# Values of a window-attention block made channel-major, turned in 32x32 blocks and passed through DRAM

## Chip, cores and metric

One Trainium2 chip, one of its cores. The metric is the device time of one execution in microseconds; the median of three runs of the kernel before is 2936.64 us.

## Reference, cut to what matters

A Swin block on x of shape (16, 192, 56, 56) in float32: layer norm over the 192 channels, cyclic shift by 3, windows of 7x7 = 49 tokens, attention with 6 heads of 32 channels, projection, second layer norm, an MLP with a hidden width of 768, and the input added at the end.

```python
qkv = jnp.einsum('bnc,oc->bno', xw, qkv_w) + qkv_b
qkv = qkv.reshape(Bw, N, 3, HEADS, dh)
q, k, v = (qkv[:, :, 0], qkv[:, :, 1], qkv[:, :, 2])
attn = jnp.einsum('bnhd,bmhd->bhnm', q, k) * scale
attn = jax.nn.softmax(attn, axis=-1)
out = jnp.einsum('bhnm,bmhd->bnhd', attn, v).reshape(Bw, N, C)
out = jnp.einsum('bnc,oc->bno', out, proj_w) + proj_b
```

## The kernel before

The work is cut into 128 units, each one row of eight windows: 8 x 49 = 392 tokens (T), four pairs of windows with 98 tokens (TP) each. Every engine runs a written-out loop over steps `t`; in each step it works on several units at once, `u[lag]` being unit `t - lag`. The order inside a step is fixed by hand in the `step` function of each engine, and semaphores tie the engines together. TensorE starts a unit (lag 0) with the products of queries, keys and values. The labels of the steps differ by engine: VectorE takes the values of a unit out of PSUM at its lag 3, while SyncE moves them at its lag 4 and GpSimd's lags are one lower than VectorE's.

To keep float32 precision, each operand is a high part in fp32r and a low part that is the rest. A product of 192 input channels is then five products: `x_h` with high and low weights, `x_l` with high weights, and the tile `x_r` (the last 64 channels' high part on partitions 0 to 63, their low part on 64 to 127) with `w_rh` and `w_rl`. `five` (lines 325 to 329) has the channels of the output on partitions and 392 columns; `five_tokens` (lines 335 to 339) has the 98 tokens of a pair on partitions and 192 columns. The values use `five_tokens`, four times a unit, 20 products in all, in the PSUM banks `vt` 0 and 1.

VectorE copies the values from PSUM to the tile `vs` in two instructions (`v_out`, line 1071): [98 tokens, pair, 192 channels]. SyncE's `spread` (line 453) moves them from `vs` to `vbd` in four transfers, for each window of a pair and each head of a pair of heads. Each has 49 partitions and runs of 32 floats, so 49 x 12 = 588 runs of 128 bytes. `vbd` holds blocks with the tokens of one head on partitions 0 to 48 and those of the next on 64 to 112, each beside zeros. `weighted` (line 607), the last work of TensorE's step, reads it one step later.

All transfers of the steady state are issued by SyncE, in this order in its step t:

```python
load_groups(t)      # xg, line 395
stats_in(t - 2)     # bc from DRAM, line 412
spread(t - 4)       # vbd, line 453
stats_out(t - 1)    # mean_rstd to DRAM, lines 404, 405; waits for GpSimd
store(t - 7)        # out, lines 419, 420; waits for GpSimd's residual
load(...)           # xt, lines 386, 387
```

GpSimd's step, in order: `scaled_probs(3)`, `hidden_lo_last`, `scaled_probs(0)`, `rstd(0)`, `less_mean_rest` (line 1233), `times_rstd_rest` (line 1237), `rstd(1)` (lines 1222 and 1226), `scaled_probs(1)`, `residual` (line 1254), `scaled_probs(2)`. `rstd(1)` feeds VectorE's `normalise` (line 993), and `residual` releases SyncE's `store`.

Of the kernel before, what the change touches and what calls it, by code (L numbers as in the profile page):

```python
# [101 lines left out]
def swin_block_program(nc, x, n1w, n1b, qkv_wt, qkv_b, proj_wt, proj_b, n2w, n2b,  # L102
                       fc1_wt, fc1_b, fc2_wt, fc2_b, out):
    ctx = ExitStack()
    with ctx:
# [28 lines left out]
        wq = [sb(f"wq_{p}", [128, NQ], F32R) for p in ("mh", "ml", "rh", "rl")]  # L134
        wp = [sb(f"wp_{p}", [128, CR + C], F32R) for p in ("mh", "ml", "rh", "rl")]
        w1 = [sb(f"w1_{p}", [128, NF], F32R) for p in ("mh", "ml", "rh", "rl")]
        w2h = sb("w2h", [128, MT, C], F32R)
        w2l = sb("w2l", [128, MT, CM], F32R)
        w2r = sb("w2r", [128, MT, 128], F32R)
# [40 lines left out]
        half_k = sb("half_k", [128, 2])  # L180
        bk = sb("bk", [128, 2])

        vbd = sb("vbd", [128, 2, 2, PAIRS, 3, WP])
        vs = sb("vs", [TP, 2, PAIRS, C])
# [52 lines left out]
        s_vs = sem("values_in_sbuf")  # L237
# [58 lines left out]
        def last_read(name, i, v):  # L296

            if name in ("x2", "o"):
                return s_lo[name], v, 3, 2 * i
            if name == "ln2":  # L300
                return s_norm, v, PAIRS, 2 * i + 1
            if name == "vt":
                return s_vs, v, 2, i
# [76 lines left out]
        def _(sp):  # L380
# [59 lines left out]
            sp.dma_start(b2[:, 0:1], fc2_b[0:CM].rearrange("(p a) -> p a", a=1)).then_inc(s_rest, 16)  # L440
            sp.dma_start(b2[0:CR, 1:2], fc2_b[CM:C].rearrange("(p a) -> p a", a=1)).then_inc(s_rest, 16)

            def spread(u):

                sp.wait_ge(s_vs, nth(u, 2, 1))
                if u > 1:

                    sp.wait_ge(s_pe["o"], nth(u - 2, 1, 0))
                src = vs[:, u % 2].rearrange("p j (a e d) -> p (j a) e d", a=3, e=2)
                dst = vbd[:, u % 2].rearrange("p i j a d -> p i (j a) d")  # L450
                for wi in range(2):
                    for e in range(2):
                        sp.dma_start(dst[WP * e:WP * e + N, wi, :, DH * e:DH * e + DH],
                                     src[N * wi:N * wi + N, :, e, :]).then_inc(s_vbd[u % 2], 16)

            for t in range(UNITS + 7):
                if t < UNITS:
                    if t > 2:
                        load_groups(t)
                    if 1 < t < AHEAD:  # L460
                        load(0, t)
                if 0 <= t - 2 < UNITS:
                    if t - 2 > 0:
# [24 lines left out]
        def _(pe):  # L488
# [102 lines left out]
            def weighted(u, j):  # L591
                if j == 0:
                    pe.wait_ge(s_vbd[u % 2], nth(u // 2, VMOVES, VMOVES - 1))
                    claim(u, [("o", 0), ("o", 1)], (s_ptc, PAIRS, 0))
                else:
                    claim(u, [], (s_ptc, PAIRS, j))


                for wi, p in ((0, 0), (0, 1), (1, 0), (1, 1), (0, 2), (1, 2)):
                    if p < 2:  # L600
                        w = 2 * j + wi
                        ps = bank("o", 0)[WP * p:WP * p + WP, N * w:N * w + N]
# [4 lines left out]
                    last = nc.tensor.matmul(ps, vbd[0:KP, u % 2, wi, j, p, :], pt[:, j, block, N * side:N * side + N],  # L607
                                            start=True, stop=True)
                if j == PAIRS - 1:
                    last.then_inc(s_pe["o"], 1)  # L610
# [5 lines left out]
                if u == 0 and tile == 4:  # L616
                    hidden_bias_products()

            def values(u, j):
                c, cc = j // 2, j % 2  # L620
                if cc == 0:
                    claim(u, [("vt", c)], (s_lo["x1"], 2, 1))
                pairs = [p[:, TP * j:TP * j + TP] for p in x1]
                last = five_tokens(bank("vt", c)[0:TP, cc * C:(cc + 1) * C], wq, pairs)
                if cc == 1:
                    last.then_inc(s_pe["vt"], 1)

            def step(t, k, it):
                u = units(t)
                if u[0] is not None:  # L630
                    values(u[0], 0)
                if u[4] is not None:
                    fc2_lo(u[4], 3)
                if u[0] is not None:
# [2 lines left out]
                    fc2_lo(u[4], 4)  # L637
                    fc2_lo(u[4], 5)
                if u[0] is not None:
                    values(u[0], 1)  # L640
                    values(u[0], 2)
                if u[3] is not None:
                    fc1(u[3], 0)
                if u[0] is not None:
                    values(u[0], 3)
                if u[3] is not None:
                    fc1(u[3], 1)
                if u[0] is not None:
# [237 lines left out]
        def _(dve):  # L886
# [9 lines left out]
            def split(n, w, raw, cols, nw, scaled):  # L896
# [14 lines left out]
                dve.wait_ge(s_scaled, scaled)  # L911
                nc.vector.tensor_tensor(w[1][:, :], sm_[:, 0:cols], w[0][:, :].bitcast(F32), ALU.subtract)

                low = CR if n == 1 else 128
                nc.vector.tensor_tensor(w[3][0:low, :], sr_[0:low, 0:cols], w[2][0:low, :].bitcast(F32), ALU.subtract).then_inc(s_split, 1)
                return scaled
# [149 lines left out]
            def v_out(u, c):  # L1066
                if u > 1:

                    dve.wait_ge(s_vbd[u % 2], nth(u // 2 - 1, VMOVES, VMOVES - 1))
                dve.wait_ge(s_pe["vt"], nth(u, 2, c))  # L1070
                nc.vector.tensor_copy(vs[:, u % 2, 2 * c:2 * c + 2, :], bank("vt", c)[0:TP, 0:2 * C].rearrange("p (j n) -> p j n", j=2)).then_inc(s_vs, 1)

            def step(t, k, it):
                u = units(t)
# [95 lines left out]
                if u[3] is not None:  # L1170
                    less_max(u[3], 0)
                    row_max(u[3], 1)
                if u[5] is not None:
# [5 lines left out]
                if u[2] is not None:  # L1179
                    if u[2] > 0:  # L1180
                        lo_part("x1", u[2], 1)
                if u[3] is not None:
                    row_max(u[3], 2)
                if u[0] is not None:
# [23 lines left out]
        def _(pool):  # L1208
# [30 lines left out]
            def hidden_lo_last(u):  # L1239
# [16 lines left out]
            def step(t, k, it):  # L1256
# [10 lines left out]
                if u[1] is not None:  # L1267
                    if u[1] > 0:
                        less_mean_rest(u[1], (k - 1) % SLOTS)
                    if u[1] > 0:  # L1270
                        times_rstd_rest(u[1])
                if u[4] is not None:
                    rstd(1, u[4])
                if u[3] is not None:
# [35 lines left out]
```

## Time and profile before

| | |
|---|---|
| median of three runs | 2936.64 us (2935.59 to 3475.99) |
| profiled execution | 2936.91 us |
| its span in the trace | 2935.1 us |
| TensorE busy | 2889.1 us (98%) |
| VectorE busy | 2629.3 us (90%) |
| ScalarE busy | 2690.1 us (92%) |
| GpSimd busy | 1363.0 us (46%) |

The profiled execution is 0.3 us from the median. Its span is the time between the first and the last record of the trace; 1.8 us of the execution lie around it. A busy share is the share of the span in which an engine had an instruction under way; the chain of work that ended last says which engine's work set the end. The DMA share is the mean busy share of the core's 16 DMA engines.

### The profile page before, as it was taken

Reading aid. Unit: us, or ns where it says so; the run is one execution under the profiler, and the core shown is the slowest. Engines: PE = TensorE matmul, PEld = TensorE weight load, DVE = VectorE, ACT = ScalarE, POOL = GpSimd, SP = SyncE. Lnnn points to the kernel's source line nnn. Section 1 sums busy time; section 2 is a strip of 40 time slices with the busy share of each in tenths; the row PEclk is TensorE's granted clock in tenths of the full one; section 3 lists DMA queues with packets and bytes.
Section 4 is the critical chain, followed back from the end, with each engine's and each line's share of the span. In section 5 each row is a group of like instructions: output and inputs, shape, how many; then the busy total and the mean of one; then the engine's idle time right before and its main releaser. Section 6 shows DMA issues by size and latency. Waiting matters only on the chain.

```text
span 2935.1 us, 74792 instructions
## 1 busy us (share of the span) xinstructions
PE 2889.1 (98%) x26284; PEld 2820.0 (96%) x26284; DVE 2629.3 (90%) x7211; ACT 2690.1 (92%) x5500; POOL 1363.0 (46%) x1549
## 2 busy tenths in 40 slices
PE   5999999999999999999999999999999999999998
PEld 5999999999999999999999999999999999999998
DVE  7899999999999999999999999999999999999985
ACT  2899999999999999999999999999999999999996
POOL 3444444444445444444444444444445444444442
PEclk9999999999999999999999999999999999999999
DMA  5333333333333333333333333333333333333321
GB/s 110 56 78 76 71 71 76 77 68 76 79 70 71 74 79 68 74 78 72 68 76 80 68 72 78 74 68 76 80 69 72 76 77 67 76 73 75 69 62 26
DMA packets 645586, 213.10 MB, mean 73 GB/s; under 512 B 500835, under 2 KB 628580, under 8 KB 645220
## 3 DMA queue, kind: packets, MB, share of 16 engines
q1 hardware_dynamic: 641284, 206.65, 32.2%
q8 instruction: 217, 3.56, 0.6%
q10 hardware_dynamic: 3936, 1.68, 0.3%
q14 instruction: 149, 1.22, 0.2%
HBM read 130.69 MB, written 38.94 MB: 58 GB/s over the span
## 4 chain that ended last, share of the span: by engine, by line
PE 97%; SPq 1%; DVE 1%; DMA 0%; POOL 0%; ACT 0%; issue 0%; POOLq 0%; DVEq 0%; ACTq 0%
PE psum L325 7%; PE psum L329 7%; PE psum L327 7%; PE psum L328 7%; PE psum L326 7%; PE psum L607 7%; PE psum L581 6%; PE psum L561 5%; PE psum L572 5%; PE psum L562 5%; PE psum L563 5%; PE psum L573 5%; PE psum L587 4%; PE psum L335 4%; PE psum L337 3%; PE psum L339 3%
## 5 line engine op out<-in xcount | busy, mean ns | idle before, releaser
L1249 POOL TENSOR_TENSOR pr<-pr,rc 98x294 f32<-98x294 f32 x512 | 386.4, 764 | 378.3 <-DVE rc L1064 378.3
L763 ACT ACTIVATE hh<-psum,b 128x392 fp32r<-128x392 f32 x768 | 451.5, 588 | 43.3 <-PE psum L573 34.7
L766 ACT ACTIVATE hf<-psum,b 128x392 f32<-128x392 f32 x768 | 451.4, 588 | 6.3
L1222 POOL TENSOR_TENSOR ve<-mv,eps 104x4 f32<-104x4 f32 (+1 forms) x256 | 80.9, 316 | 759.8 <-DVE mv L988 759.8
L1243 POOL TENSOR_TENSOR hl<-hf,hh 128x392 fp32r<-128x392 f32 x128 | 224.0, 1750 | 370.5 <-ACT hf L766 370.5
L1028 DVE TENSOR_TENSOR hl<-hf,hh 128x392 fp32r<-128x392 f32 x640 | 347.9, 559 | 4.0 <-ACT hf L766 4.0
L1051 DVE TENSOR_REDUCE mx<-psum 98x6 f32<-98x294 f32 x512 | 232.2, 454 | 128.4 <-PE psum L582 124.5
L561 PE MATMUL psum<-hh,w2h 128*128 128x392 f32 x768 | 272.1, 354 | 0.0
L325 PE MATMUL psum<-x_h,w_mh 128*128 128x392 f32 x768 | 270.2, 352 | 0.7 <-DVE pr L1056 0.7
L581 PE MATMUL psum<-km,qm 128*98 128x98 f32 x2048 | 262.5, 251 | 7.7 <-DVE xn L993 3.4
L720 ACT ACTIVATE pt<-psum 113x294 f32<-113x294 f32 x512 | 206.3, 403 | 69.2 <-PE psum L587 69.0
L572 PE MATMUL psum<-hl,w2h 128*128 128x392 f32 x768 | 264.4, 344 | 0.3 <-POOL hl L1243 0.3
L329 PE MATMUL psum<-x_r,w_rl 128*128 128x392 f32 x768 | 262.7, 342 | 0.0
L327 PE MATMUL psum<-x_l,w_mh 128*128 128x392 f32 x768 | 262.0, 341 | 0.0
L562 PE MATMUL psum<-hh,w2l 128*128 128x392 f32 x768 | 262.0, 341 | 0.0
L328 PE MATMUL psum<-x_r,w_rh 128*128 128x392 f32 x768 | 260.9, 340 | 0.0
L326 PE MATMUL psum<-x_h,w_ml 128*128 128x392 f32 x768 | 260.8, 340 | 0.0
L573 PE MATMUL psum<-hl,w2h 128*64 128x392 f32 x768 | 259.8, 338 | 0.0
L563 PE MATMUL psum<-hh,w2r 128*128 128x392 f32 x768 | 259.2, 338 | 0.0
L980 DVE BATCH_NORM_STATS2 st<-psum 98x6 f32<-98x192 f32 x512 | 184.0, 359 | 74.8 <-PE psum L339 70.7
L581 PEld LDWEIGHTS psum<-km,qm 128*98 128x98 f32 x2048 | 238.5, 167 | 12.4 <-issue 6.3
L1056 DVE TENSOR_TENSOR pr<-psum,mx 98x294 f32<-98x294 f32 x512 | 234.1, 457 | 4.2
(144 smaller groups left out, 10394.9 us busy)
## 6 DMA issues: line engine op xcount, KB each, us to landing
bc<-mean_rstd SPq DMA_DIRECT2D x128, 392.0 KB, 3.7
vbd<-vs SPq DMA_DIRECT2D x512, 73.5 KB
xg<-in_x SPq DMA_DIRECT2D x368, 96.0 KB, 2.5
xt<-in_x SPq DMA_DIRECT2D x112, 194.5 KB, 2.7
out<-xt SPq DMA_DIRECT2D x112, 194.5 KB, 1.9
xt<-in_x SPq DMA_DIRECT2D x112, 97.2 KB, 2.5
out<-xt SPq DMA_DIRECT2D x112, 97.2 KB, 2.1
mean_rstd<-mv SPq DMA_DIRECT2D x384, 1.0 KB
```

Of the source, the lines that this page charges most:

```text
L325: nc.tensor.matmul(ps, wmh[:, c0:c0 + m], xh, start=True, stop=False)
L326: nc.tensor.matmul(ps, wml[:, c0:c0 + m], xh, start=False, stop=False)
L327: nc.tensor.matmul(ps, wmh[:, c0:c0 + m], xl, start=False, stop=False)
L328: nc.tensor.matmul(ps, wrh[:, c0:c0 + m], xrr, start=False, stop=False)
L329: return nc.tensor.matmul(ps, wrl[:, c0:c0 + m], xrr, start=False, stop=True)
L561: nc.tensor.matmul(ym, w2h[:, m, 0:CM], hh[:, b, :], start=a, stop=False)
L562: nc.tensor.matmul(ym, w2l[:, m, :], hh[:, b, :], start=False, stop=False)
L572: nc.tensor.matmul(ym, w2h[:, m, 0:CM], hl[:, b, :], start=False, stop=z)
L573: nc.tensor.matmul(yx[0:CR], w2h[:, m, CM:C], hl[:, b, :], start=False, stop=z, skip_group_check=True).then_inc(s_pe["fc2"], 1)
L581: nc.tensor.matmul(ps[:, TP * wi:TP * wi + TP], qm[:, w, :], km[:, w, :], start=True, stop=True)
L763: nc.scalar.activation(hh[:, m % HB, :], bank("fc1", m)[:, 0:T], ACT.Gelu, bias=b1[:, m:m + 1]).then_inc(s_hh, 1)
L766: nc.scalar.activation(hf[:, m % HB, :], bank("fc1", m)[:, 0:T], ACT.Gelu, bias=b1[:, m:m + 1]).then_inc(s_gelu, 1)
```

## The change

The values are computed with channels on partitions. `values_rest` makes the last 64 channels in three products: a weight tile `wv_m` holds the high weights in its columns 0 to 63 and the low ones in 64 to 127, `wv_r` likewise, so that the partitions 0 to 63 of the result have one part of the sum and 64 to 127 the other. `values_main` makes the first 128 channels with `five`. That is eight products of 392 columns.

VectorE no longer copies: `v_out` turns 32x32 blocks from PSUM to SBUF (`vt_r`, then `vt_m`), [128 channels, 8 windows, 2 blocks of 32 tokens]. A window has 49 tokens, so its second block begins at token 17 and repeats 15 of them. After it the partition within a block is the token and the last dimension the channel of a head.

SyncE's `low_part` moves the lower half of `vt_r` to `vt_l` on partitions 0 to 63. GpSimd's `last_values` adds it. `values_to_dram` writes both tiles to a DRAM tensor `by_token`, and `spread` reads `vbd` from it one step later, in four transfers: for each head of a pair, 32 tokens and then the 17 that are left. Each moves runs of 128 bytes, as before: 32 x 24 = 768 runs and 17 x 24 = 408.

In VectorE's step, `lo_part("x1", 1)` (line 1022, `x_r`) moves ahead of `lo_part("x2", 0)`, `less_max(1)` and `hidden_lo(4)`. In SyncE's step `low_part(t - 3)` follows `spread(t - 4)`, and `values_to_dram(t - 3)` follows `stats_out(t - 1)`.

```diff
             def spread(u):
-                sp.wait_ge(s_vs, nth(u, 2, 1))
+                sp.wait_ge(s_vd, 16 * 2 * (u + 1))
                 if u > 1:
                     sp.wait_ge(s_pe["o"], nth(u - 2, 1, 0))
-                src = vs[:, u % 2].rearrange("p j (a e d) -> p (j a) e d", a=3, e=2)
-                dst = vbd[:, u % 2].rearrange("p i j a d -> p i (j a) d")
-                for wi in range(2):
-                    for e in range(2):
-                        sp.dma_start(dst[WP * e:WP * e + N, wi, :, DH * e:DH * e + DH],
-                                     src[N * wi:N * wi + N, :, e, :]).then_inc(s_vbd[u % 2], 16)
+                of_pair = by_token[u % 2].rearrange("(p e t) w b d -> e b t w p d", p=3, e=2)
+                for e in range(2):
+                    dst = vbd[:, u % 2, :, :, DH * e:DH * e + DH]
+                    sp.dma_start(dst[WP * e:WP * e + DH], of_pair[e, 0]).then_inc(s_vbd[u % 2], 16)
+                    sp.dma_start(dst[WP * e + DH:WP * e + N], of_pair[e, 1, 2 * DH - N:DH]).then_inc(s_vbd[u % 2], 16)
...
+            def low_part(u):
+                sp.wait_ge(s_vt, nth(u, 2, 0))
+                if u > 0:
+                    sp.wait_ge(s_vsum, nth(u - 1, 1, 0))
+                sp.dma_start(vt_l[:, :, :, :], vt_r[CR:128, u % 2]).then_inc(s_vlow, 16)
+            def values_to_dram(u):
+                sp.wait_ge(s_vt, nth(u, 2, 1))
+                if u > 1:
+                    sp.wait_ge(s_vbd[u % 2], 16 * 4 * (u // 2))
+                sp.dma_start(by_token[u % 2, 0:CM], vt_m[:, u % 2]).then_inc(s_vd, 16)
+                sp.wait_ge(s_vsum, nth(u, 1, 0))
+                sp.dma_start(by_token[u % 2, CM:C], vt_r[0:CR, u % 2]).then_inc(s_vd, 16)
...
                 if 0 <= t - 4 < UNITS:
                     spread(t - 4)
+                if 0 <= t - 3 < UNITS:
+                    low_part(t - 3)
...
                         stats_out(t - 1)
+                if 0 <= t - 3 < UNITS:
+                    values_to_dram(t - 3)
...
+            def values_main(u):
+                claim(u, [("vt", 1)])
+                five(bank("vt", 1)[:, 0:T], wq, 0, CM, [p[:, :] for p in x1]).then_inc(s_pe["vt"], 1)
+            def values_rest(u):
+                claim(u, [("vt", 0)], (s_lo["x1"], 2, 0))
+                ps = bank("vt", 0)[:, 0:T]
+                nc.tensor.matmul(ps, wv_m[:, :], x1[0][:, :], start=True, stop=False)
+                nc.tensor.matmul(ps, wv_m[:, :], x1[1][:, :], start=False, stop=False)
+                pe.wait_ge(s_lo["x1"], nth(u, 2, 1))
+                nc.tensor.matmul(ps, wv_r[:, :], x1[2][:, :], start=False, stop=True).then_inc(s_pe["vt"], 1)
...
                 dve.wait_ge(s_pe["vt"], nth(u, 2, c))
-                nc.vector.tensor_copy(vs[:, u % 2, 2 * c:2 * c + 2, :], bank("vt", c)[0:TP, 0:2 * C].rearrange("p (j n) -> p j n", j=2)).then_inc(s_vs, 1)
+                blocks = bass.AP(psum, BANK_OF["vt", c] * 512, [[8 * 512, 128], [N, NW], [N - DH, 2], [1, DH]])
+                nc.vector.transpose((vt_r, vt_m)[c][:, u % 2], blocks).then_inc(s_vt, 1)
...
+            def last_values(u):
+                pool.wait_ge(s_vlow, 16 * (u + 1))
+                nc.gpsimd.tensor_tensor(vt_r[0:CR, u % 2], vt_r[0:CR, u % 2], vt_l[:, :, :, :], ALU.add).then_inc(s_vsum, 1)
...
                     if u[1] > 0:
                         times_rstd_rest(u[1])
+                if u[2] is not None:
+                    last_values(u[2])
                 if u[4] is not None:
                     rstd(1, u[4])
```

In TensorE's step, `values_rest` stands where the first pair of the values stood, `values_main` where the second and third stood, and the fourth is gone. VectorE makes `wv_m` and `wv_r` once, in the prologue, with four small instructions. `weighted` reads `vbd` by window instead of by pair and window.

## Rows read from the trace of the kernel before

**Rows 1.** The page: busy time of each engine, and the last chain by engine.

```profile
PE 2889.1 (98%) x26284; PEld 2820.0 (96%) x26284; DVE 2629.3 (90%) x7211; ACT 2690.1 (92%) x5500; POOL 1363.0 (46%) x1549
...
PE 97%; SPq 1%; DVE 1%; DMA 0%; POOL 0%; ACT 0%; issue 0%; POOLq 0%; DVEq 0%; ACTq 0%
```

**Rows 2.** The last chain in order of time: start, length, what; one unit apart.

```profile
1741.03 1.54 PE psum L607 x48
1763.41 1.54 PE psum L607 x48
```

**Rows 3.** Waits: engine and line, releaser: us in total, times, longest.

```profile
POOL ve L1222 <- DVE mv L988: 759.8, 255, 12.1
...
DVE mx L1051 <- PE psum L582: 124.5, 125, 2.2
DVE st L980 <- PE psum L339: 70.7, 134, 1.9
```

**Rows 4.** Waits of the SyncE queue, same columns.

```profile
SPq L417 <- POOL xt L1254: 948.4, 128, 16.1
```

**Rows 5.** Timeline of TensorE, 1500 to 1524: start us, length us, operation.

```profile
1500.64 0.25 PE L335 MATMUL psum<-wq_mh,x_h 128*98 128x192 f32 x1
...
1501.09 0.36 PE L325 MATMUL psum<-x_h,w_mh 128*128 128x392 f32 x1
...
1502.00 0.34 PE L325 MATMUL psum<-x_h,wq_mh 128*128 128x392 f32 x1
...
1502.89 0.25 PE L335 MATMUL psum<-wp_mh,o_h 128*98 128x192 f32 x1
```

**Rows 6.** Timeline of VectorE, 1500 to 1530; idle time before in brackets.

```profile
1500.59 0.53 DVE L1071 COPY vs<-psum 98x384 f32<-98x384 f32 x1
...
1502.53 0.97 DVE L959 STREAM_TRANSPOSE xtok<-xg 128x768 f32<-128x768 f32 x1
1503.98 0.37 DVE L980 BATCH_NORM_STATS2 st<-psum 98x6 f32<-98x192 f32 x1 [0.49 <-PE psum L339]
...
1513.35 0.47 DVE L1051 TENSOR_REDUCE mx<-psum 98x6 f32<-98x294 f32 x1 [1.00 <-PE psum L582]
...
1515.25 0.57 DVE L1022 TENSOR_TENSOR x_l<-psum,x_h 128x392 fp32r<-128x392 f32 x1 [0.21 <-ACT x_h L720]
...
1516.69 1.26 DVE L1022 TENSOR_TENSOR x_r<-yr,x_r 64x392 fp32r<-64x392 f32 x1
...
1520.43 0.75 DVE L999 TENSOR_TENSOR x_r<-psum,x_r 64x196 fp32r<-64x196 f32 x2
```

**Rows 7.** Timeline of VectorE in the prologue.

```profile
53.55 0.56 DVE L1022 TENSOR_TENSOR x_r<-yr,x_r 64x392 fp32r<-64x392 f32 x1
```

**Rows 8.** Timeline of GpSimd, 1500 to 1530.

```profile
1503.14 1.04 POOL L1237 TENSOR_TENSOR yr<-yr,bc 64x392 f32<-64x392 f32 x1
1507.93 0.43 POOL L1222 TENSOR_TENSOR ve<-mv,eps 98x4 f32<-98x4 f32 x1 [3.76 <-DVE mv L988]
...
1510.27 1.02 POOL L1254 TENSOR_TENSOR xt<-yr,xt 64x392 f32<-64x392 f32 x1
```

**Rows 9.** Windows of 0.5 us: length, GpSimd busy, PEclk, DMA share, GB/s.

```profile
1519.00:1519.50 0.50, 0.00 (x0) 1.00 0.80 196
...
1521.00:1521.50 0.50, 0.11 (x1) 1.00 0.66 270
...
1523.50:1524.00 0.50, 0.50 (x1) 1.00 0.55 85
...
1528.00:1528.50 0.50, 0.00 (x0) 1.00 0.00 0
```

**Rows 10.** DMA issues: count, KB each, median us to landing.

```profile
bc<-mean_rstd SPq DMA_DIRECT2D x128, 392.0 KB, 3.7
vbd<-vs SPq DMA_DIRECT2D x512, 73.5 KB
xg<-in_x SPq DMA_DIRECT2D x368, 96.0 KB, 2.5
```

**Rows 11.** Timeline of the SyncE queue, 1480 to 1530: start, issue time, transfer.

```profile
1488.98 0.36 SPq L419 DMA_DIRECT2D out<-xt  x1
...
1496.65 4.85 SPq L453 DMA_DIRECT2D vbd<-vs  x4
...
1511.36 0.36 SPq L419 DMA_DIRECT2D out<-xt  x1
...
1520.31 3.77 SPq L453 DMA_DIRECT2D vbd<-vs  x4
```

More of the change, by code:

```diff
@@ L136, in swin_block_program @@
         w1 = [sb(f"w1_{p}", [128, NF], F32R) for p in ("mh", "ml", "rh", "rl")]
+        wv_m = sb("wv_m", [128, 128], F32R)
+        wv_r = sb("wv_r", [128, 128], F32R)
         w2h = sb("w2h", [128, MT, C], F32R)
@@ L181, in swin_block_program @@
         bk = sb("bk", [128, 2])
-        vbd = sb("vbd", [128, 2, 2, PAIRS, 3, WP])
-        vs = sb("vs", [TP, 2, PAIRS, C])
+        vbd = sb("vbd", [128, 2, NW, 3, WP])
+        vt_m = sb("vt_m", [128, 2, NW, 2, DH])
+        vt_r = sb("vt_r", [128, 2, NW, 2, DH])
+        vt_l = sb("vt_l", [CR, NW, 2, DH])
+        by_token = nc.dram_tensor("values_by_token", [2, C, NW, 2, DH], F32)
         pr = sb("pr", [TP, PAIRS, HEADS * WP])
@@ L236, in swin_block_program @@
         s_qkv = sem("qkv_in_sbuf")
-        s_vs = sem("values_in_sbuf")
+        s_vt = sem("values_by_token")
+        s_vlow = sem("low_part_of_last_values_moved")
+        s_vsum = sem("last_values_summed")
+        s_vd = sem("values_in_dram")
         s_vbd = [sem(f"vbd_ready_{i}") for i in range(2)]
@@ L302, in last_read @@
             if name == "vt":
-                return s_vs, v, 2, i
+                return s_vt, v, 2, i
             if name == "qkv":
@@ L606, in weighted @@
                     block, side = (wi, p) if p < 2 else (2, wi)
-                    last = nc.tensor.matmul(ps, vbd[0:KP, u % 2, wi, j, p, :], pt[:, j, block, N * side:N * side + N],
+                    last = nc.tensor.matmul(ps, vbd[0:KP, u % 2, 2 * j + wi, p, :], pt[:, j, block, N * side:N * side + N],
                                             start=True, stop=True)
@@ L617, in qkv @@
                     hidden_bias_products()
[L619 to L626, printed above, removed]
+            def values_main(u):
[8 more added lines that the diff above has]
+                nc.tensor.matmul(ps, wv_r[:, :], x1[2][:, :], start=False, stop=True).then_inc(s_pe["vt"], 1)
             def step(t, k, it):
@@ L630, in step @@
                 if u[0] is not None:
-                    values(u[0], 0)
+                    values_rest(u[0])
                 if u[4] is not None:
@@ L639, in step @@
                 if u[0] is not None:
-                    values(u[0], 1)
-                    values(u[0], 2)
+                    values_main(u[0])
                 if u[3] is not None:
                     fc1(u[3], 0)
-                if u[0] is not None:
-                    values(u[0], 3)
                 if u[3] is not None:
@@ L912, in split @@
                 nc.vector.tensor_tensor(w[1][:, :], sm_[:, 0:cols], w[0][:, :].bitcast(F32), ALU.subtract)
+                if n == 0:
+                    for pair, raw_, of in ((wv_m, sm_, w[0]), (wv_r, sr_, w[2])):
+                        nc.vector.tensor_copy(pair[:, 0:CR], of[:, CM:C].bitcast(F32))
+                        nc.vector.tensor_tensor(pair[:, CR:128], raw_[:, CM:C], of[:, CM:C].bitcast(F32), ALU.subtract)
                 low = CR if n == 1 else 128
@@ L1067, in v_out @@
                 if u > 1:
-                    dve.wait_ge(s_vbd[u % 2], nth(u // 2 - 1, VMOVES, VMOVES - 1))
+                    dve.wait_ge(s_vd, 16 * 2 * (u - 1))
                 dve.wait_ge(s_pe["vt"], nth(u, 2, c))
-                nc.vector.tensor_copy(vs[:, u % 2, 2 * c:2 * c + 2, :], bank("vt", c)[0:TP, 0:2 * C].rearrange("p (j n) -> p j n", j=2)).then_inc(s_vs, 1)
+                blocks = bass.AP(psum, BANK_OF["vt", c] * 512, [[8 * 512, 128], [N, NW], [N - DH, 2], [1, DH]])
+                nc.vector.transpose((vt_r, vt_m)[c][:, u % 2], blocks).then_inc(s_vt, 1)
             def step(t, k, it):
@@ L1172, in step @@
                     row_max(u[3], 1)
+                if u[2] is not None:
+                    if u[2] > 0:
+                        lo_part("x1", u[2], 1)
                 if u[5] is not None:
@@ L1178, in step @@
                     hidden_lo(u[6], 4)
-                if u[2] is not None:
-                    if u[2] > 0:
-                        lo_part("x1", u[2], 1)
                 if u[3] is not None:
@@ L1271, in step @@
                         times_rstd_rest(u[1])
+                if u[2] is not None:
+                    last_values(u[2])
                 if u[4] is not None:
```

## The prediction

> **What bounds the kernel now.** I read the page first: TensorE is busy for 98% of the span, and 97% of the chain that ended last is its work [rows 1]. Then the chain in time: `weighted` comes back after exactly 22.38 us (1763.41 - 1741.03) [rows 2], so 128 units make 2865 us, and some 70 us are prologue and drain. TensorE hardly waits for anybody. The waits tell who has room: VectorE waits 124.5 us for scores and 70.7 us for the projection, some 1.5 us a unit; GpSimd waits 759.8 us for VectorE's means [rows 3]; SyncE's queue waits 948.4 us, 7.4 us a unit, for GpSimd's `residual` [rows 4]. The first question is what TensorE saves, the second whether anything that the change puts behind SyncE, GpSimd or a DMA engine makes a loop longer than 22.38 us.
>
> **What TensorE saves.** In the steady pitch five products of 192 columns take 0.45 us (1501.09 - 1500.64) and five of 392 columns 0.89 us (1502.89 - 1502.00) [rows 5]: 0.090 and 0.178 us each. 20 x 0.090 = 1.80 us of values become 8 x 0.178 = 1.42. That is 0.38 us a unit, 48 us in all; a little of the changeover between narrow and wide products goes too (0.91 instead of 0.89 us for the wide group behind a narrow one [rows 5]), so up to 56 us. If nothing else bound, the period would be 22.0 us.
>
> **VectorE.** Two copies of 384 elements (0.53 us [rows 6]) become two block turns of 512. The nearest row is the turn of 768 elements from SBUF, 0.97 us [rows 6]; in proportion 0.65, and at most 0.97 if PSUM is slower. So +0.1 to +0.45 each; I take +0.15, and 0.3 a unit. VectorE's idle time in one step is 0.49 + 1.00 + 0.21 = 1.70 us [rows 6]; 0.4 of it goes with TensorE's shorter period, 0.3 (at most 0.9) with the turns. 0.4 us or more are left: it doesn't become the bound. Moving `x_r` forward costs nothing and may give 0.7 us back: the same instruction takes 1.26 us in the steady state, behind GpSimd's work on `hl`, but 0.56 us in the prologue [rows 6, 7], and in its new place it would start before that work. It delays three instructions by 0.6 to 1.3 us; `x_r` on line 999, which follows all three, keeps its time at 1521.2 [rows 6]. `values_main` takes over its PSUM bank at just about that time; a stall of 0 to 0.2 us a unit there is possible, and I take 0. The four instructions in the prologue are 1 us.
>
> **GpSimd.** `last_values` adds 64x512 elements; line 1237 adds 64x392 in 1.04 us [rows 8], so 1.04 x 512/392 = 1.36 us. It stands in a gap of 3.76 us between 1504.2 and 1507.9 [rows 8] and is free if its data are there by about 1506.5. If they aren't, `rstd(1)`, the probabilities and `residual` are queued behind it on GpSimd; `normalise` on VectorE waits for the first, SyncE's `store` for the last.
>
> **The read-back, the term that decides.** Before, each of the four transfers has 49 partitions. A stretch in which hardly anything else moves shows them at 85 GB/s and a DMA share of 0.55, where the `xg` transfers (32 partitions) reach 196 GB/s and 0.80 [rows 9]. So 49 partitions don't use all 16 DMA engines. If a transfer is cut into equal groups of partitions over at most 16 engines, 49 = 7 x 7 goes to seven. Then the pace is 85 GB/s / 128 bytes / 7 = 95 runs a microsecond on an engine, 10.5 ns a run, while the record of a run lasts 0.55 x 16 x 500 ns / 332 runs = 13.3 ns: neighbours overlap, which is how seven engines show a share over 7/16. Cut by the same arithmetic, 32 partitions go to 16 engines, 48 runs each; but 17 is a prime and over 16, so all its 408 runs go to one engine. Per unit that engine gets 48 + 408 + 48 + 408 = 912 runs in a row, where the busiest had 336 before. The number of runs and of bytes stays as it was; only their spread over engines changes.
>
> The Trainium skill, "DMA: Bandwidth & Descriptors", section "Why a DMA increments its semaphore by 16 and not by 1", has this as a rule: the number of engines is the largest one up to 16 that divides the slowest dimension of both sides, and they are the lowest-numbered. The measured share and rate of 49 partitions agree with its seven; that 17 gives one, no run here shows yet. By the rule the sum is the one below; with an even spread it would be the first rival's.
>
> The price of a run read from DRAM by one engine isn't in the trace. From below it is the 10.5 ns of SBUF. From above: `xg` with runs of 512 bytes (196 GB/s, share 0.80) has 33 ns a run and `bc` with 3136 bytes (270 GB/s, 0.66) 123 ns [rows 9, 10]; a line through both gives 20.3 ns at 128 bytes, with 16 engines sharing the DRAM. I take 13.3 ns, the length of a record of the same size. 912 runs last 9.6, 12.1 or 18.5 us.
>
> **Why that isn't hidden.** `vbd` itself has time: `weighted` stands at the end of the step. But `low_part` is issued behind `spread` on the same queue, and a share of it goes over the crowded engine, behind the 912 runs. So there is a loop of SyncE, that engine and GpSimd:
>
> - from `store`'s first issue to `spread`'s first: 20.31 - 11.36 = 8.95 us in one step, 96.65 - 88.98 = 7.67 in the one before [rows 11]; 8.3.
> - from the issue to the first runs, with the `bc` transfer in front: the pure stretch at 1523.50 is already under way at 1523.0 or before, issue at 1520.31 [rows 9, 11]; 2.5.
> - the 912 runs: 12.1 (9.6 to 18.5).
> - `low_part`'s own rows and its landing: an estimate of 0.8 from transfers that land 2.5 us after their issue [rows 10], most of which is gone by then.
> - `last_values`: 1.36.
> - GpSimd from `rstd(1)` to the end of `residual`, and `store`'s issue: 11.36 - 7.93 = 3.43 [rows 8, 11].
>
> Sum: 8.3 + 2.5 + 12.1 + 0.8 + 1.36 + 3.43 = 28.5 us (26.0 to 34.9), over 22.38 and over 22.0. The wait for `residual`, 7.4 us a unit [rows 4], is the slack that it eats, and the saving of TensorE doesn't show. If SyncE can't hand over 408 runs to one engine at once, `low_part` is issued up to 2 us later, within the range. The other three additions (the writes to DRAM in rows of 2048 bytes, their waits) stand behind `low_part`; `values_to_dram` waits for the sum, which comes 3.4 us ahead of the release of `store`, and has landed long before the next `spread`.
>
> Against the profiled execution (span 2935.1, 2936.9 in all, the median's 2936.6): 127 x (28.5 - 22.38) = 777, so 3714; I say 3710. With 26.0 it is 3400, with the shorter SyncE stretch and landing 3250; with 34.9 4530.
>
> **Rivals.**
> - *The 17 partitions are spread.* If they go over several engines as evenly as 49 do, the read-back takes 2352 runs at 85 GB/s, 3.5 us, `low_part` lands by 1505 in the frame of the rows, and all is hidden: TensorE's saving alone counts, 2937 - 52 = 2885. For it: nothing in the rows shows how 17 are cut. Against: the low share of 49. This is the case on the other side; it decides if the runs on the busiest engine last under about 5 us (22.0 - 16.4 = 5.6 us for the whole stretch).
> - *The added step isn't hidden even so.* With spread transfers, but `low_part` landing after 1506.5, `last_values` pushes `rstd(1)` back by up to its 1.36 us; VectorE's remaining 1.0 us takes most of it. 128 x 0.4 on top of 2885 is 2936.
> - *DRAM is dearer than the line.* At 25 ns a run 22.8 us, period 39.2 us, 2937 + 127 x 16.8 = 5070. For it: all these reads hit DRAM in pieces of 128 bytes. Against: the line through two rows stays under it although 16 engines shared the DRAM there.
>
> **Chances.** Forecast (one engine, 10 to 21 ns) 0.74; spread and hidden 0.11; spread and late 0.05; dearer DRAM 0.10. The range 3250 to 4700 takes the forecast with its bounds and the near edge of the last case, and leaves the two spread cases and the far edge out. A measurement of this kernel can tell 2% from no change: faster by more than 2% would be under 2878, which only the spread case could reach with a changeover gain: 0.04. Within 2%: 0.12. Slower: 0.84.
>
> **What would show it.** Right: TensorE with an idle stretch in each step and a period of 26 to 35 us; GpSimd waiting at `last_values` for a DMA; a stretch of some 10 us in each unit with a DMA share near 1/16 (0.06 to 0.1) and about 10 GB/s; VectorE waiting for GpSimd's `rs`. The number of products of 392 columns up by 1024, those of 192 down by 2560, at the same pitch. Turns of about 0.65 us. Wrong: if the share stays near 0.55 during `spread`, the step about one engine fails; if the share is low but GpSimd doesn't wait, the step about the order on the queue does. The prediction would also be off if TensorE's clock fell in its idle stretches, which the rows, with a granted clock of 1.00 throughout [rows 9], don't show.

## The result, and the profile after

| | before | after |
|---|---|---|
| median | 2936.11 us | 3278.9 us |
| ratio | | 1.117, 95% interval 1.116 to 1.118 |
| span of the profiled execution | 2935.1 us | 3280.7 us |
| period of a unit | 22.38 us | 25.1 us (mean) |

One of the four runs of the kernel before took 3475.99 us and is left out of the ratio; the others lie between 2934 and 2937. The change makes the kernel 343 us slower. The forecast was 3710 us (774 more), with a range of 3250 to 4700. The whole difference is in the period: 127 x (25.12 - 22.38) = 348 us.

The page of the kernel after, the busy times and the chain that ended last by engine; they answer to [rows 1].

```profile
PE 2961.8 (90%) x24748; PEld 2824.3 (86%) x24748; DVE 2740.6 (84%) x7215; ACT 2693.7 (82%) x5500; POOL 1344.3 (41%) x1677
...
SPq 53%; DMA 21%; POOL 16%; PE 5%; issue 5%; ACT 0%; DVE 0%; POOLq 0%; DVEq 0%; ACTq 0%
```

TensorE's work of the last chain has gone from 97% to 5%. The set of things that now follow on one another is SyncE's queue, a DMA and GpSimd. The waits of the engines and then of SyncE's queue say the same; they answer to [rows 3, 4].

```profile
POOL vt_r L1292 <- DMA vt_l<-vt_r: 774.8, 126, 8.1
...
DVE xn L1033 <- POOL rs L1270: 339.7, 123, 5.4
```

```profile
SPq L428 <- POOL xt L1303: 326.9, 127, 13.0
SPq L470 <- POOL vt_r L1292: 109.1, 121, 2.4
```

GpSimd waits 774.8 us, 6.1 us a unit, for the low part to land, and behind it VectorE waits 340 us for `rs`. SyncE's wait for `residual` has shrunk from 948.4 us to 326.9. So the loop that the prediction names is there. One turn of it in SyncE's timeline (start, issue time, transfer), which answers to [rows 11]:

```profile
1504.22 0.64 SPq L481 DMA_DIRECT2D vbd<-values_by_token  x1
1504.91 0.68 SPq L482 DMA_DIRECT2D vbd<-values_by_token  x1
1505.64 4.31 SPq L481 DMA_DIRECT2D vbd<-values_by_token  x1
1509.99 0.64 SPq L482 DMA_DIRECT2D vbd<-values_by_token  x1
1510.73 3.58 SPq L460 DMA_DIRECT2D vt_l<-vt_r  x1
...
1520.41 0.35 SPq L430 DMA_DIRECT2D out<-xt  x1
...
1530.43 0.63 SPq L481 DMA_DIRECT2D vbd<-values_by_token  x1
```

The lines 481 are the transfers of 32 partitions, 482 those of 17, 460 is the low part. The transfer behind each one of 17 partitions takes 4.31 and 3.58 us to issue, where its like takes 0.64 and some 0.5; I call the extra time a hold. GpSimd in the same stretch, to be held against [rows 8]:

```profile
1516.19 1.28 POOL L1292 TENSOR_TENSOR vt_r<-vt_r,vt_l 64x512 f32<-64x512 f32 x1 [5.63 <-DMA vt_l<-vt_r]
1517.43 0.19 POOL L1266 TENSOR_TENSOR ve<-mv,eps 98x4 f32<-98x4 f32 x1
...
1519.33 1.00 POOL L1303 TENSOR_TENSOR xt<-yr,xt 64x392 f32<-64x392 f32 x1
```

The sum starts at 1516.19, 1.9 us after the low part's issue has ended, and `rstd(1)` (line 1266), the probabilities and `residual` (line 1303) follow without a gap; `store` is issued at 1520.41. Taken over some 100 turns between 200 and 2750 us, the three stretches are, from `store` to the first read-back 8.80 us, from there to the sum 12.05, from the sum to `store` 4.27: together 25.12, the period.

The windows of 1 us (length, TensorE busy, PEclk, DMA share, GB/s), which answer to [rows 9]:

```profile
1508.00:1509.00 1.00, 1.00 (x8) 1.00 0.09 14
1509.00:1510.00 1.00, 1.00 (x10) 1.00 0.09 14
1510.00:1511.00 1.00, 1.00 (x13) 1.00 0.20 33
1511.00:1512.00 1.00, 1.00 (x9) 1.00 0.55 86
1512.00:1513.00 1.00, 1.00 (x11) 1.00 0.09 14
...
1515.00:1516.00 1.00, 1.00 (x8) 1.00 0.68 129
...
1543.00:1544.00 1.00, 0.73 (x5) 1.00 0.64 246
1544.00:1545.00 1.00, 0.00 (x0) 1.00 0.00 0
1545.00:1546.00 1.00, 0.25 (x2) 0.91 0.21 55
1546.00:1547.00 1.00, 1.00 (x8) 0.50 0.42 92
...
1549.00:1550.00 1.00, 1.00 (x8) 0.89 0.28 45
```

Between two transfers of 32 partitions (the 0.55 at 1511) the share is 0.09 and the rate 14 GB/s. I read that as the crowded engine alone: 128 bytes / 14 GB/s = 9.1 ns a run. The profile doesn't name the DMA engines; the experiments below vary how many runs one of them would get. In windows of 0.25 us the 14 GB/s last until 1510.5, and until 1514.75 behind the second transfer of 17 partitions, so each held issue (to 1509.95 and to 1514.31) ends about 0.5 us or more before the last of the runs.

### The profile page after: what moved, and what is told of

Same layout as the page of the kernel before. It is cut to its first block, busy times and chain, and to the rows that moved or that the text cites. A ratio compares the mean times of both kernels' runs of the same rounds, so it can differ in the third digit from the quotient of the medians.

```text
span 3280.7 us, 72362 instructions
## 1 busy us (share of the span) xinstructions
PE 2961.8 (90%) x24748; PEld 2824.3 (86%) x24748; DVE 2740.6 (84%) x7215; ACT 2693.7 (82%) x5500; POOL 1344.3 (41%) x1677
## 3 DMA queue, kind: packets, MB, share of 16 engines
q14 instruction: 155, 1.27, 0.2%
## 4 chain that ended last, share of the span: by engine, by line
SPq 53%; DMA 21%; POOL 16%; PE 5%; issue 5%; ACT 0%; DVE 0%; POOLq 0%; DVEq 0%; ACTq 0%
DMA vt_l<-vt_r 21%; SPq L481 18%; SPq L406 10%; SPq L397 5%; SPq L482 5%; POOL vt_r L1292 5%; SPq L431 4%; SPq L398 4%; SPq L430 4%; POOL rs L1270 4%; POOL xt L1303 4%; POOL pr L1298 2%; SPq L423 2%; POOL ve L1266 1%; PE psum L639 0%
## 5 line engine op out<-in xcount | busy, mean ns | idle before, releaser
L1298 POOL TENSOR_TENSOR pr<-pr,rc 98x294 f32<-98x294 f32 x512 | 344.0, 681 | 490.3 <-DVE rc L1104 490.3
L1033 DVE TENSOR_SCALAR xn<-psum,mv,rs 98x192 f32<-98x192 f32 x512 | 218.5, 469 | 339.8 <-POOL rs L1270 339.7
L1292 POOL TENSOR_TENSOR vt_r<-vt_r,vt_l 64x512 f32<-64x512 f32 x128 | 168.0, 1312 | 774.8 <-DMA vt_l<-vt_r 774.8
L613 PE MATMUL psum<-km,qm 128*98 128x98 f32 x2048 | 284.0, 264 | 146.2 <-DVE xn L1033 137.3
L1068 DVE TENSOR_TENSOR hl<-hf,hh 128x392 fp32r<-128x392 f32 x640 | 369.1, 577 | 24.0 <-ACT hf L801 13.3
L639 PE MATMUL psum<-pt,vbd 113*64 113x49 f32 x6144 | 206.1, 223 | 95.7 <-DVE pr L1096 95.7
L639 PEld LDWEIGHTS psum<-pt,vbd 113*64 113x64 f32 x6144 | 192.6, 138 | 111.6 <-issue 107.9
L593 PE MATMUL psum<-hh,w2h 128*128 128x392 f32 x768 | 281.7, 367 | 0.0
L619 PE MATMUL psum<-ident,pr 98*128 98x98 f32 x1536 | 232.0, 264 | 40.5 <-POOL pr L1298 39.7
```

Of the source, the lines that this page charges most:

```text
L593: nc.tensor.matmul(ym, w2h[:, m, 0:CM], hh[:, b, :], start=a, stop=False)
L613: nc.tensor.matmul(ps[:, TP * wi:TP * wi + TP], qm[:, w, :], km[:, w, :], start=True, stop=True)
L639: last = nc.tensor.matmul(ps, vbd[0:KP, u % 2, 2 * j + wi, p, :], pt[:, j, block, N * side:N * side + N], start=True, stop=True)
L1068: nc.vector.tensor_tensor(hl[:, b, :], hf[:, b, :], hh[:, b, :].bitcast(F32), ALU.subtract).then_inc(s_hl, 1)
L1292: nc.gpsimd.tensor_tensor(vt_r[0:CR, u % 2], vt_r[0:CR, u % 2], vt_l[:, :, :, :], ALU.add).then_inc(s_vsum, 1)
L1298: nc.gpsimd.tensor_tensor(probs(j), probs(j), each, ALU.mult).then_inc(s_prob, 1)
```

## Experiments

In the table, "middle" is the mean time from the first read-back issue to the sum on GpSimd, and "SyncE's work" the period less its waits for semaphores, so its issues and whatever holds them. Both are worked out from the timelines and waits of each profile; "busiest" counts the 128-byte runs of a unit on the busiest engine, by equal groups of partitions; it is worked out and not read from a profile. A single partition is counted by its next dimension, the 8 windows, which no run measures by itself (with all of it on one engine the 150 would be 192, the 531 552). Where the low part goes ahead of the read-back, the middle no longer holds all of the read-back. The diffs leave out the semaphore increments and counts and the conditions around calls.

| kernel | busiest | period | middle | SyncE's work | time | ratio to before |
|---|---|---|---|---|---|---|
| before | 336 | 22.38 | | 14.2 | 2936 | 1 |
| after | 912 | 25.12 | 12.05 | 21.6 | 3279 | 1.117 |
| 32, 16 and 1 | 150 | 22.12 | 6.95 | 16.2 | 2910 | 0.991 (0.9895 to 0.9925) |
| low part first | 912 | 22.68 | 4.81 | 21.7 | 2982 | 1.017 (1.015 to 1.018) |
| 31 and 18 | 1584 | 31.4 | 18.43 | | 4069, one run | |
| before, cut at 32 | 912 | 22.38 | | 20.2 | 2943, one run | |
| no low part | 912 | 22.22 | | 21.5 | 2913 | 0.992 (0.990 to 0.994) |
| both cures | 150 | 22.14 | 2.53 | | 2909 | 0.991 (0.989 to 0.992) |
| old place of x_r | 150 | 22.63 | 7.04 | | 2973 | 1.013 (1.011 to 1.014) |
| one seventeen | 531 | 23.23 | 9.79 | 19.4 | 3052 | 1.040 (1.038 to 1.042) |
| behind the means | 912 | 23.64 | 3.30 | 22.9 | 3093 | 1.053 (1.052 to 1.055) |
| before, x_r early | 336 | | | | 2937 | 1.0006 (0.9996 to 1.0015) |
| seventeens apart | 912 | 23.64 | 6.16 | 22.9 | 3095 | 1.054 (1.052 to 1.056) |

**Is it the 17 partitions?** The read-back in 32, 16 and 1 partitions:

```diff
-    sp.dma_start(dst[WP * e + DH:WP * e + N], of_pair[e, 1, 2 * DH - N:DH])
+    sp.dma_start(dst[WP * e + DH + 1:WP * e + N], of_pair[e, 1, 2 * DH - N + 1:DH])
+    sp.dma_start(dst[WP * e + DH:WP * e + DH + 1], of_pair[e, 1, 2 * DH - N:2 * DH - N + 1])
```

> The changed kernel with the read-back cut into 32, 16 and 1 partitions per head instead of 32 and 17: the same runs of 128 bytes, two more transfers a unit. Theory (the 816 runs of the two 17-partition transfers go over one DMA engine, and the low part waits behind them): no engine has more than some 150 runs in a row, the 12.05 us between the first read-back issue and the sum on GpSimd fall to 5 or 6, the loop of 8.8 + 6 + 4.3 = 19 us is shorter than TensorE's step, period 22.0 to 22.4, time 2885 to 2930. Rival (short reads from DRAM are dear on whatever engines): the stretch stays near 12 us and the time at 3279. Rival (the added round trip and sum are dear by themselves): 3150 or more.

2909.56 us: 369 us less than the changed kernel, with the same runs and two more transfers, and 0.9% faster than before. SyncE's timeline of this kernel:

```profile
1507.84 0.63 SPq L481 DMA_DIRECT2D vbd<-values_by_token  x1
1508.52 0.66 SPq L482 DMA_DIRECT2D vbd<-values_by_token  x1
1509.22 0.71 SPq L483 DMA_DIRECT2D vbd<-values_by_token  x1
...
1512.13 0.53 SPq L460 DMA_DIRECT2D vt_l<-vt_r  x1
...
1521.04 0.36 SPq L430 DMA_DIRECT2D out<-xt  x1
```

No issue is held: 0.63, 0.66, 0.71, and 0.53 for the low part, which the sum follows at 1514.51, 1.85 us after the issue has ended, as in the changed kernel. So neither short reads from DRAM nor the added round trip is dear by itself.

**The slope.** 31 and 18 partitions instead of 32 and 17:

```diff
-    sp.dma_start(dst[WP * e:WP * e + DH], of_pair[e, 0])
-    sp.dma_start(dst[WP * e + DH:WP * e + N], of_pair[e, 1, 2 * DH - N:DH])
+    sp.dma_start(dst[WP * e:WP * e + DH - 1], of_pair[e, 0, 0:DH - 1])
+    sp.dma_start(dst[WP * e + DH - 1:WP * e + N], of_pair[e, 1, 2 * DH - N - 1:DH])
```

> The changed kernel with the read-back cut into 31 and 18 partitions per head. 31 is a prime too, so 744 runs each would go over one engine, and 18 over nine: 1584 runs in a row on the busiest engine instead of 912, with as many runs in all. Theory, at the 9.1 ns a run that the profile of the change shows: 672 x 9.1 ns = 6.1 us more a unit, period 31.2 us, time near 4055. Rival (the number of runs in all counts, or their size): 3279.

4069 us against 4055 expected; the middle is 6.4 us longer, 672 runs x 9.5 ns. SyncE's timeline (481: 31 partitions, 482: 18):

```profile
1520.35 0.73 SPq L481 DMA_DIRECT2D vbd<-values_by_token  x1
1521.13 7.40 SPq L482 DMA_DIRECT2D vbd<-values_by_token  x1
1528.59 0.66 SPq L481 DMA_DIRECT2D vbd<-values_by_token  x1
1529.29 6.96 SPq L482 DMA_DIRECT2D vbd<-values_by_token  x1
```

744 runs x 9.1 ns are 6.8 us. Here a transfer of 18 partitions carries the hold of the one before it, 7.40 and 6.96 us, for an issue of 0.7. The same count of runs and bytes gives 2910, 3279 or 4069 us, by the number of partitions of a transfer (the first has two transfers more). That the groups are equal and 31 and 17 go to one engine explains all three. (The kernel with 31 and 18 ran once.)

**SBUF or DRAM?** The kernel before, with its moves cut the same way:

```diff
-    sp.dma_start(dst[WP * e:WP * e + N, wi, :, DH * e:DH * e + DH],
-                 src[N * wi:N * wi + N, :, e, :]).then_inc(s_vbd[u % 2], 16)
+    for a, z in ((0, DH), (DH, N)):
+        sp.dma_start(dst[WP * e + a:WP * e + z, wi, :, DH * e:DH * e + DH],
+                     src[N * wi + a:N * wi + z, :, e, :]).then_inc(s_vbd[u % 2], 16)
```

> The kernel before with its moves from SBUF cut into 32 and 17 partitions: eight transfers instead of four, 912 runs in a row on one engine, and no GpSimd step behind them. Theory: hidden, 2936 within 1%; the windows show a DMA share of 0.09. Their rate is the price of a run from SBUF: 14 GB/s (9.1 ns) if DRAM is no dearer than SBUF, over it if DRAM is dearer. Rival (one crowded engine delays the whole queue): 3000 or more.

2943 us in one run, with the period at 22.38 us as before. Windows of 0.5 us (length, PEclk, DMA share, GB/s):

```profile
1507.50:1508.00 0.50, 1.00 0.09 14
1508.00:1508.50 0.50, 1.00 0.09 14
```

14 GB/s from SBUF too: a run from DRAM takes no longer. And the kernel before has room for all of it, though SyncE's work rises from 14.2 to 20.2 us a unit.

**Who waits: the place in the queue.** The low part ahead of the read-back:

```diff
+                if 0 <= t - 3 < UNITS:
+                    low_part(t - 3)
                 if 0 <= t - 4 < UNITS:
                     spread(t - 4)
-                if 0 <= t - 3 < UNITS:
-                    low_part(t - 3)
```

> The changed kernel with the low part issued ahead of the read-back on SyncE's queue; the 17-partition transfers stay. Theory: the crowded engine still works 8.3 us a unit (DMA share 0.09 at 14 GB/s), but nothing that GpSimd needs stands behind it, so the loop is open: period 22.0 to 22.4, time 2885 to 2940. Rival (the read-back is itself late for the weighted sums, or delays the next unit's loads and means): 3000 or more.

2982 us, a miss: most of the loss is gone, but 72 us stay over 2910. GpSimd now waits 349 us for the broadcast means instead of the 46 of the changed kernel. I took it for their place behind the runs and put the read-back behind the means' writes as well:

```diff
-                spread(t - 4)
                 low_part(t - 3)
                 stats_out(t - 1)
+                spread(t - 4)
```

> The changed kernel with the read-back (17-partition transfers kept) issued behind the low part and behind the means' way to DRAM. With the low part alone in front the time was 2982, and GpSimd waited 349 us for the broadcast means, whose writes stood behind the runs. Theory (the crowded engine costs only what stands behind it): with the means in front too, that wait falls under 80 us and the time to 2905 to 2935. Rival (SyncE's queue itself is full, since it is held 4 us by one such transfer): 2960 or more, with SyncE no longer waiting for GpSimd's residual.

3093 us: worse, the rival. The wait for the means grew to 488 us. SyncE's timeline, the second 17 and what follows it:

```profile
1524.80 0.63 SPq L482 DMA_DIRECT2D vbd<-values_by_token  x1
1525.54 3.62 SPq L468 DMA_DIRECT2D values_by_token<-vt_m  x1
```

and SyncE's waits of the same run:

```profile
SPq L428 <- POOL xt L1303: 38.8, 4, 13.5
```

SyncE hardly waits for `residual` any longer (38.8 us in all): its queue is the bound. The values' write to DRAM, 0.34 us of issue otherwise, takes 3.62. So the hold isn't on the low part; it falls on whatever SyncE issues next. The 72 us of the reordering before this one aren't isolated by any run: SyncE's work is 21.7 us of 22.68 there, and the first write of the means is the issue that is held, up to 3.9 us.

**Half of the cure.** Only the second head's 17 partitions become 16 and 1:

```diff
-    sp.dma_start(dst[WP * e + DH:WP * e + N], of_pair[e, 1, 2 * DH - N:DH])
+    if e == 0:
+        sp.dma_start(dst[WP * e + DH:WP * e + N], of_pair[e, 1, 2 * DH - N:DH])
+    else:
+        sp.dma_start(dst[WP * e + DH + 1:WP * e + N], of_pair[e, 1, 2 * DH - N + 1:DH])
+        sp.dma_start(dst[WP * e + DH:WP * e + DH + 1], of_pair[e, 1, 2 * DH - N:2 * DH - N + 1])
```

> Only the second head of a pair read back in 32, 16 and 1 partitions; the first keeps 32 and 17. The busiest engine has 531 runs instead of 912, 3.5 us less at 9.1 ns. By the sum of the loop: 8.8 + (12.05 - 3.5) + 4.3 = 21.7 us, just under TensorE's 22.1, so 2910 to 2935: half of the cure gives nearly all of the gain. If each 17-partition transfer costs its share whatever the bound: near 3095, half of the way from 3279 to 2910.

3052 us, a miss: the sum of the loop had the wrong middle, 8.6 instead of 9.79, and 4.3 instead of 4.7 behind it. I had taken off 381 runs x 9.1 ns = 3.5 us. The held issue of one turn:

```profile
1514.13 3.82 SPq L485 DMA_DIRECT2D vbd<-values_by_token  x1
```

Its median over the run is 4.05 us, 3.4 more than the 0.62 of its like. By holds the table nearly adds up: 6.95 with none, + 3.4 for one held issue - 0.7 for one issue less is 9.65 (9.79 measured). In the changed kernel the two held issues take 4.07 and 3.69 us on average, 3.4 and 3.2 over their own, so 6.95 + 6.6 - 1.4 is 12.15 (12.05 measured).

**Cutting the loop elsewhere.** Without `low_part` and `last_values`; the values of the last 64 channels lack their low part:

```diff
-                if 0 <= t - 3 < UNITS:
-                    low_part(t - 3)
...
-                sp.wait_ge(s_vsum, nth(u, 1, 0))
...
-                if u[2] is not None:
-                    last_values(u[2])
```

> The changed kernel, 17-partition transfers kept, without the low part's move and without its sum on GpSimd, so the values of the last 64 channels lack their low part. Theory (the crowded engine costs time only through what GpSimd waits for behind it): 912 runs still take 8.3 us on one engine, but the loop is cut; TensorE bounds, period 22.1 us as with 32, 16 and 1 partitions, 2900 to 2920. Rival (the crowded queue delays loads, means or the values themselves, as it did to the means when the low part went first): 2960 or more.

2913 us with all 912 runs on one engine. So with the loop over GpSimd cut in this way the time is 4 us over that of 32, 16 and 1 partitions, not 369. (That kernel still has the low part and its sum; a kernel without either and with 32, 16 and 1 wasn't run.) But SyncE's work is 21.5 us of 22.2: it is nearly full.

**Both cures, and the holds apart.** The read-back in 32, 16 and 1 (the first diff) with the low part ahead of it (the diff of the low part first):

> Read-back in 32, 16 and 1 partitions, and the low part ahead of it. Theory (TensorE bounds already with the first edit): 2900 to 2915, no gain over 2910. Rival (what is left of GpSimd's wait for the low part, 124 us, costs time): 2885 to 2895.

2909 us: nothing more to gain there. Then the same four transfers as in the changed kernel, the two of 17 partitions issued apart:

```diff
                 for e in range(2):
-                    dst = vbd[:, u % 2, :, :, DH * e:DH * e + DH]
-                    sp.dma_start(dst[WP * e:WP * e + DH], of_pair[e, 0])
-                    sp.dma_start(dst[WP * e + DH:WP * e + N], of_pair[e, 1, 2 * DH - N:DH])
+                    sp.dma_start(vbd[WP * e:WP * e + DH, u % 2, :, :, DH * e:DH * e + DH], of_pair(u)[e, 0])
...
+            def seventeen(u, e):
+                sp.dma_start(vbd[WP * e + DH:WP * e + N, u % 2, :, :, DH * e:DH * e + DH],
+                             of_pair(u)[e, 1, 2 * DH - N:DH])
...
+                if 0 <= t - 4 < UNITS:
+                    seventeen(t - 4, 0)
                 if 0 <= t - 3 < UNITS:
                     values_to_dram(t - 3)
+                if 0 <= t - 4 < UNITS:
+                    seventeen(t - 4, 1)
```

> The changed kernel with the same four read-back transfers, 912 runs on one engine as before, but the two of 17 partitions issued apart and late: one behind the means' way to DRAM, one behind the values' way to DRAM, just ahead of the wait for the residual; the low part stands behind the two of 32 only. Theory now (what costs is that SyncE can't issue its next transfer until the 408 runs of one engine are through, 3.3 us each time, and everything behind it comes late): the low part is issued without such a hold, one hold falls partly into the wait for the sum and one into the wait for the residual, so 2905 to 2940. Rival (912 runs on one engine cost their time wherever they stand, as in the two reorderings before): 2980 or more.

3095 us, a miss. SyncE's timeline:

```profile
1525.35 0.67 SPq L485 DMA_DIRECT2D vbd<-values_by_token  x1
1526.13 4.86 SPq L468 DMA_DIRECT2D values_by_token<-vt_m  x1
...
1531.57 0.66 SPq L485 DMA_DIRECT2D vbd<-values_by_token  x1
1533.53 2.52 SPq L430 DMA_DIRECT2D out<-xt  x1
```

The values' write is held until 1530.99, `store` until 1536.05. Apart, a hold is longer than 3.3 us: the values' write takes 5.2 us in the median. Behind the issue of the 17 partitions come some 2 us until the first run (1526.02 to 1528.1) and then 3.7 us of runs; in the changed kernel, so I take it, part of that latency passes while other transfers are issued. SyncE is full (it waits 0.7 us a unit), VectorE waits 52 us for the loaded `xg`, and TensorE waits for `vbd` as well (87 us). That the wait for `residual` would swallow the hold was wrong: with 22.9 us of work SyncE has none left.

**x_r, in both kernels.** First in the old place, with the read-back in 32, 16 and 1:

```diff
                 row_max(u[3], 1)
-                lo_part("x1", u[2], 1)
                 lo_part("x2", u[5], 0)
                 less_max(u[3], 1)
                 hidden_lo(u[6], 4)
+                lo_part("x1", u[2], 1)
                 row_max(u[3], 2)
```

> Read-back in 32, 16 and 1 partitions, and the low part of x_r back in its old place in VectorE's order. Theory (VectorE has room): 2910 within 0.3%, with this instruction at 1.26 us again instead of 0.56. Rival (the move carries part of the gain, since the products of the last 64 channels wait for it): 2920 to 2960, with TensorE waiting for x_r.

2973 us, 63 more than with the move: the rival, though over its 2960 and not by its reason. TensorE, and below it VectorE:

```profile
1523.50 0.34 PE L340 MATMUL psum<-x_r,wq_rl 128*128 128x392 f32 x1
1524.17 0.30 PE L346 MATMUL psum<-wp_mh,o_h 128*98 128x192 f32 x1 [0.33 <-DVE vt_m L1116]
```

and VectorE of the same run:

```profile
1515.41 1.27 DVE L1063 TENSOR_TENSOR x_r<-yr,x_r 64x392 fp32r<-64x392 f32 x1
```

TensorE doesn't wait for `x_r` but for the turn of `vt_m`, 0.33 us in each step by the profile; from product to product it is 0.67 us instead of 0.18, 0.49 of the 0.51 us by which the period grew: `project` (line 346) needs the PSUM bank that `v_out(1)` reads. VectorE's stretch from the first `row_max` to that turn has no idle time but 0.21 us, and carries the 1.27 us of `x_r` and the longer turns. Then the move alone, in the kernel before:

```diff
                 row_max(u[3], 1)
+                lo_part("x1", u[2], 1)
                 lo_part("x2", u[5], 0)
                 less_max(u[3], 1)
                 hidden_lo(u[6], 4)
-                lo_part("x1", u[2], 1)
```

> The kernel before with one edit: the low part of x_r in the place that the change gives it. Its duration should fall from 1.26 to about 0.56 us. TensorE's chain bounds that kernel without waiting, so theory: 2936 within 0.3%. Rival (the move is a gain by itself, as it was with the turned values): 2900 to 2925.

2937 us, no difference, with `x_r` at 0.56 us as expected. It is worth 63 us only where the turns have used up the room.

## Why the prediction was wrong in size

**Right: the cut and the loop.** The step that 17 partitions go to one engine is borne out by the three kernels with 150, 912 and 1584 runs on the busiest engine and by the share of 0.09; the loop of SyncE, a DMA and GpSimd is the chain of the profile, and leaving the sum out opens it. The rule that the text took beside it from the Trainium skill ("DMA: Bandwidth & Descriptors", section "Why a DMA increments its semaphore by 16 and not by 1": the largest count up to 16 that divides the slowest dimension) agrees with what the runs show: a DMA share of 0.09 at 14 GB/s for 17 and for 31 partitions, and no hold for 16.

**The term that was mis-sized: "The 912 runs: 12.1 (9.6 to 18.5)".** A run costs 9.1 ns, so they take 8.3 us, under the end that I had called the lower one. The forecast period was 28.5 us and the measured one 25.12; of these 3.4 us the runs account for 3.8, and the other terms together gave back 0.4. I had taken the length of a run's record, 13.3 ns, though the same paragraph says that records overlap; on one engine they overlap as well (0.09 x 16 x 128 bytes / 14 GB/s = 13.2 ns a record, 9.1 a run). The lower end, 10.5 ns, was the rate of seven engines under four issues, and no bound. The upper end, by a line through the reads from DRAM, was a price of DRAM that isn't there: the cut in the kernel before shows the same 9.1 ns from SBUF.

With 8.3 in its place the middle would be 2.5 + 8.3 + 0.8 = 11.6 us (measured 12.05), and the loop 8.3 + 11.6 + 4.8 = 24.7 (25.12). The other terms were 8.3 for 8.80 and 4.79 for 4.27, since `rstd(1)` takes 0.19 + 1.01 us, with VectorE idle meanwhile, where it took 0.43 + 1.21. 127 x (24.7 - 22.38) = 295 on top of 2937 gives 3232 us.

That 3279 us lies inside the range of 3250 to 4700 is luck. The runs measured outside their own bounds (8.3 against 9.6 to 18.5 us), and the 3250 came from a shorter SyncE stretch (7.67 us) and a shorter landing, while that stretch measured 8.80.

**The place of the wait was wrong.** "A share of it goes over the crowded engine, behind the 912 runs": the sum starts 1.9 us after the low part's issue has ended, with or without the crowd. What comes late is the issue, since SyncE doesn't get the next transfer out until most of the 408 runs are through. I had that as a side remark of up to 2 us; the two holds are 3.4 and 3.2. It makes little difference to the changed kernel's sum, but two repairs by order failed by it (3093 and 3095 us, with 22.9 of 23.64 us taken up by SyncE's issues and holds). What inside the queue the next transfer waits for, the profile doesn't show.

**TensorE's saving** is 0.26 us a unit by the period (22.38 - 22.12) and 0.27 by its products, not 0.38. The products of the values in the kernel with 32, 16 and 1 partitions:

```profile
1506.39 0.45 PE L662 MATMUL psum<-x_h,wv_m 128*128 128x392 f32 x1
...
1507.03 0.34 PE L605 MATMUL psum<-hl,w2h 128*128 128x392 f32 x1
...
1509.00 0.34 PE L336 MATMUL psum<-x_h,wq_mh 128*128 128x392 f32 x1
...
1509.89 0.34 PE L336 MATMUL psum<-x_h,w_mh 128*128 128x392 f32 x1
```

The last 64 channels take 0.64 us (1507.03 - 1506.39), as the first product behind `weighted` has a pitch of 0.28, and the first 128 take 0.89: 1.53 instead of 1.80. With this saving the first rival's 2885 us would have been 2903 (2937 - 127 x 0.27); the kernel with the read-back spread took 2910.

**VectorE "doesn't become the bound"** held for the whole step and not for its tightest stretch. The turns take, in the kernel after:

```profile
1506.97 0.68 DVE L1115 STREAM_TRANSPOSE vt_r<-psum 128x512 f32<-128x512 f32 x1
...
1508.59 0.72 DVE L1115 STREAM_TRANSPOSE vt_m<-psum 128x512 f32<-128x512 f32 x1
```

0.68 and 0.72 us against 0.53 for a copy [rows 6], inside the bounds. But I weighed them against 1.70 us of idle time of a step, 1.49 of which lies where it doesn't help. The move of `x_r`, costed at nothing, is what keeps the kernel with 32, 16 and 1 partitions from being slower than before (2910 against 2973 us). The 0.7 us that it "may give" back came there, and not in the changed kernel, where GpSimd's `hl` runs beside the new place too:

```profile
1523.46 1.03 POOL L1287 TENSOR_TENSOR hl<-hf,hh 128x392 fp32r<-128x392 f32 x1 [1.84 <-ACT hf L801]
```

```profile
1523.67 1.23 DVE L1062 TENSOR_TENSOR x_r<-yr,x_r 64x392 fp32r<-64x392 f32 x1
```

Its median is 1.22 us in the changed kernel and 0.56 with 32, 16 and 1.

## What to carry to other kernels

Count the partitions of each transfer of many short runs: with 17 and with 31, primes over 16, all its pieces went over one DMA engine (as the share of 0.09 and the times are read here), and the queue that issued it was held until most of them were through, whatever stood next in it. Where the queue has room and no loop passes through it that costs next to nothing (2943 us, in one run, in the kernel before); where one does it cost 369 us. Split such a transfer into 16 and a rest rather than moving it in the order. And weigh an added instruction against the idle time between the two events that it lies between, not against that of the step.

## What was not expected of the hardware

- Seven engines under four issues of 588 runs moved 85 GB/s, 10.5 ns a run, one engine alone 14 GB/s, 9.1 ns. Whether the issue or the engines set either rate wasn't tried.
- A transfer to one engine is itself issued in 0.68 us with 408 runs, and the next is held 3.2 to 5 us on average, by what stands around it, and less where SyncE waits for something else meanwhile; after one with 744 runs it is 6.2 to 6.7, after one with 204 (the kernel before, cut at 32) 0.8 to 0.9.
- In the kernel before `x_r`'s subtraction takes 1.27 us while GpSimd works on `hl`, 0.56 when it is moved ahead of it; GpSimd's own instruction takes 1.76 us in the first case and 1.03 in the second. In the changed kernel, where `hl` starts 0.2 us ahead of `x_r`, only the subtraction is longer: 1.22 us, with `hl` at 1.02.
- In the kernel after, TensorE stood idle from 1543.7 to 1545.7, and the granted clock was 0.50 (1.2 GHz) from 1546 to 1549 and 0.89 in the next window (the windows above). Over the span the mean is 0.976, against 0.997 before. TensorE is 5% of the last chain, so that cost little; it wasn't tried by itself.
